# Score pass of a graph layer: squares and weighted one-hots moved between ScalarE and VectorE

## The reference, cut to what matters

```
proj_s = feature @ W_s.T;  proj_t = feature @ W_t.T
z = proj_s[src] + proj_t[dst];  z = where(z >= 0, z, 0.2 * z)
e = (z @ W_attn.T)[:, 0]
e_exp = exp(e - m[src]);  denom = segment_sum(e_exp, src)
...
def instance_norm(t):                 # t: keys or values, 64 channels per head
    mu = mean(t, -1);  var = mean((t - mu) ** 2, -1)
    return (t - mu) * rsqrt(var + EPS)
dots = einsum('bhnd,bhne->bhde', instance_norm(k), instance_norm(v))
```

## Time and profile before

| what | us |
|---|---|
| three runs, median | 2702.7 |
| lowest and highest | 2688.93 and 2711.46 |
| the profiled execution's own time | 2693.4 |
| its span, first to last instruction | 2691.6 |
| score pass in it, first gather at 168.0, last merge at about 1552 | 1384 |

### The profile page before, as it was taken

The page is one execution under the profiler, slowest core; times in us unless marked ns, Lnnn a source line. Parts: engine busy times, 40 slices in busy tenths (PEclk is TensorE's granted clock), DMA queues, the critical chain, the costliest instruction groups (busy, mean ns, idle before and its releaser), DMA issues. The chain is left out here.

```text
span 2691.6 us, 40213 instructions
## 1 busy us (share of the span) xinstructions
PE 2176.4 (81%) x10331; PEld 1518.2 (56%) x10331; DVE 1615.4 (60%) x6311; ACT 917.9 (34%) x3931; POOL 1289.2 (48%) x1316
## 2 busy tenths in 40 slices
PE   8966776777777677767777789999999959999998
PEld 5633444444444344434444478888788846666665
DVE  7834665655666565656656668777777843334443
ACT  6731333333333333333323324444334422221111
POOL 0035556555655555555555246566556622222222
PEclk9976778787878777877778789999989969999999
DMA  7855666666666666666666467666666741222220
GB/s 227 259 182 162 182 193 186 180 191 175 191 175 199 175 184 191 186 189 176 189 179 192 118 180 246 214 212 211 201 207 213 219 167 63 78 70 72 81 71 8
DMA packets 275757, 457.24 MB, mean 170 GB/s; under 512 B 58240, under 2 KB 199842, under 8 KB 275404
## 3 DMA queue, kind: packets, MB, share of 16 engines
q0 software_dynamic: 75920, 224.24, 29.3%
q1 hardware_dynamic: 199612, 230.49, 27.7%
HBM read 346.55 MB, written 113.74 MB: 171 GB/s over the span
## 5 line engine op out<-in xcount | busy, mean ns | idle before, releaser
L832 POOL DMA_INDIRECT pool_mem<-node_tab,edges x592 | 583.4, 985 | 592.0 <-issue 326.0
L963 PE MATMUL psum<-x_all 32*128 32x258 f32 x1568 | 266.7, 506 | 226.0 <-DVE x_all L1084 120.0
L1799 PE MATMUL psum<-x_all,pool_mem 128*128 128x256 f32 x1568 | 381.3, 397 | 21.4 <-DVE pool_mem L1999 13.1
L1608 POOL DMA_INDIRECT x_all<-node_tab,edges x294 | 295.1, 1004 | 165.0 <-issue 61.2
L1799 PEld LDWEIGHTS psum<-x_all,pool_mem 128*128 128x128 f32 x1568 | 307.2, 199 | 72.4 <-DVE pool_mem L1999 14.7
L872 ACT ACTIVATE x_all<-score_all,neg_max 128x8 f32<-128x8 f32 x98 | 29.7, 303 | 807.5 <-issue 419.1
L1098 DVE TENSOR_TENSOR pool_mem<-psum,pool_mem 128x258 f32<-128x258 f32 x296 | 114.9, 421 | 301.3 <-remote 165.3
L963 PEld LDWEIGHTS psum<-x_all 32*128 32x128 f32 x1568 | 115.8, 218 | 310.1 <-DVE x_all L1084 148.8
L1091 DVE SCALAR_TENSOR_TENSOR x_all<-psum,pool_mem 128x258 f32<-128x258 f32 x392 | 155.4, 422 | 177.3 <-remote 111.4
L996 PE MATMUL psum<-wkvT,x_all 128*128 128x512 f32 x392 | 233.7, 728 | 30.1 <-remote 13.0
L832 POOL DMA_INDIRECT x_all<-node_tab,edges x192 | 189.5, 987 | 141.7 <-DMA kept_rows<-x_all 81.3
(11 more groups left out here) (258 smaller groups left out, 3870.1 us busy)
## 6 DMA issues: line engine op xcount, KB each, us to landing
x_all<-kept_rows SPq DMA_DIRECT2D x98, 640.0 KB
kept_rows<-pool_mem SPq DMA_DIRECT2D x74, 640.0 KB
x_all<-in_L_ffn_w_dram SPq DMA_DIRECT2D x16, 1024.0 KB
kept_rows<-x_all SPq DMA_DIRECT2D x24, 640.0 KB
node_tab<-pool_mem SPq DMA_DIRECT2D x49, 258.0 KB, 3.1
x_all<-proj_t SPq DMA_DIRECT2D x392, 32.2 KB
pool_mem<-node_tab,edges POOLq DMA_INDIRECT x592
moe_in<-zeros SPq DMA_DIRECT2D x32, 258.0 KB, 4.2
```

What stands on the lines that cost most here:

```text
L832: g.indirect_dma_start(source_rows(r, u, ZW + D), None, node_tab, bass.IndirectOffsetOnAxis(ap=edges[:, 0, HALF * k + u:HALF * k + u + 1], ...
L963: mm = pe.matmul(psum[:, Z_BANK[q], 0:ZW], hot_T[h][rows_q, j * P:(j + 1) * P], t_win[rows_q, h, :], start=True, stop=(pair in BY_VECTOR), ...
L1608: g.indirect_dma_start(rows_g[k % R3][:, u - KEEP, 0:n], None, node_tab, bass.IndirectOffsetOnAxis(ap=edges[:, 0, HALF * k + u:HALF * k + ...
L1799: pe.matmul(psum[:, bank, 0:D], wide_picked[:, HALF * (k % 2) + u, :], row, start=((odd == 1 or m == 0) and n == 0), stop=(n == HALF - 1 a ...
```

## The change

Three edits, all in the score pass.

1. **Weighted one-hots.** ScalarE's 8 copies with a scale (L878) are gone. VectorE makes the same 128x512 tile by one multiplication of `hi_w` with the exp values broadcast over 64 columns (`values(k)`). It stands between `weigh_sum(k + 1, 5)` and `lo_hots(k, 1)`, so ahead of `hot(k + 2)`. Waits on `s_vexp` count one per half and not eight.
2. **Squares.** ScalarE squares a whole 128x512 bank by one instruction with no sum; 16 instructions with their 16 sums per tile become 2.
3. **Sums of squares.** VectorE sums them per head by `tensor_reduce`, 128x8 from 128x512 (`head_sums`), two per tile: the keys' one at the end of an odd half, behind `hot` and ahead of the next half's first `add_row`; the values' one in step 0 of `mix_norms`, followed by a wait for its own result.

```diff
@@ ScalarE, step(k)
-                        wait(act, s_vexp, HALF * (k - 1))
+                        wait(act, s_vexp, k - 1)
                         act.activation(expo_w[h], score_all[...], ACT.Exp, bias=...).then_inc(s_exp, 1)
                         act.activation(scale_w[h], ...).then_inc(s_ex2, 1)
-                        wait(act, s_hot, 3 * k + 2)
-                        wait(act, s_tab, k - 1)
-                        wait(act, s_exp, k + 1)
-                        for u in range(HALF):
-                            act.activation(vals[h][:, u, :], hi_w[h][:, u, :], ACT.Copy, scale=expo_w[h][:, u:u + 1]).then_inc(s_vexp, 1)
@@ ScalarE, square(i, j)
-                        for q in range(HEADS):
-                            act.activation(squares_w[:, j, q * DH:(q + 1) * DH], psum[:, 4 + j, q * DH:(q + 1) * DH], ACT.Square,
-                                           accum_out=head_sq[:, j, q:q + 1]).then_inc(s_sq, 1)
+                        act.activation(squares_w[:, j, :], psum[:, 4 + j, :], ACT.Square).then_inc(s_sq, 1)
@@ TensorE, tables(k)
-                        wait(pe, s_vexp, HALF * k + HALF)
+                        wait(pe, s_vexp, k + 1)
@@ VectorE
+                    def values(k):
+                        h = k % 2
+                        wait(v, s_hot, 3 * k + 2)
+                        wait(v, s_tab, k - 1)
+                        wait(v, s_exp, k + 1)
+                        v.tensor_tensor(vals[h], hi_w[h], expo_w[h].unsqueeze(2).to_broadcast([P, HALF, HIS]), ALU.mult).then_inc(s_vexp, 1)
+
+                    def head_sums(i, j):
+                        wait(v, s_sq, 2 * i + j + 1)
+                        wait(v, s_red, i)
+                        dve.done(v.tensor_reduce(head_sq[:, j, :], squares_w[:, j, :].rearrange("p (h d) -> p h d", d=DH), AX.X, ALU.add))
@@ VectorE, mix_norms(i, 0)
-                            wait(v, s_sq, 2 * HEADS * (i + 1))
+                            head_sums(i, 1)
+                            dve.wait()
                             v.tensor_scalar(head_var, head_sq, 1.0 / DH, LN_EPS, ALU.mult, ALU.add).then_inc(s_red, 1)
@@ VectorE, the loop over k
                         mix(k, 8, 9)
+                        values(k)
                         lo_hots(k, 1)
...
                         if k % 2 == 0:
                             mix_values(k // 2)
+                        elif k // 2 + 1 < PASSES:
+                            head_sums(k // 2 + 1, 0)
```

More of the change, by code:

```diff
@@ L1127, in hi_hots @@
                         hi = attr[:, 1, HALF * k:HALF * (k + 1)].unsqueeze(2).to_broadcast([P, HALF, HIS])
-                        wait(v, s_vexp, HALF * (k - 1))
+                        wait(v, s_vexp, k - 1)
                         v.tensor_tensor(hi_w[k % 2], hi, count[:, 0:HIS].unsqueeze(1).to_broadcast([P, HALF, HIS]), ALU.is_equal).then_inc(s_hot, 1)
+                    def values(k):
[8 more added lines that the diff above has]
+                        dve.done(v.tensor_reduce(head_sq[:, j, :], squares_w[:, j, :].rearrange("p (h d) -> p h d", d=DH), AX.X, ALU.add))
                     def merge(k):
@@ L1172, in _ @@
                     hot(1)
+                    head_sums(0, 0)
                     weigh_sum(0, 0)
```

## The result

The change took 2658.1 us (median of 4 runs, 2653.1 to 2666.1), against 2695.8 for the kernel before (4 runs, 2676.9 to 2711.5). The ratio is 0.985, with a 95% interval from 0.981 to 0.989: about 40 us less, where 43 more were forecast. The time lies outside the range that was given, on the other side.

The account below looks back on a forecast made before the run. The pass was taken as bound by TensorE and VectorE waiting for each other; 35 + 21 + 9 - 8 - 14 = +43 us gave a median of 2746 us, with 8 in 10 between 2680 and 2815.

Parts of the forecast that it names:

- I cost their removal at nothing: Removing ScalarE's 8 scaled copies, 2.02 us a half, gains 0 us, since they lie off the path.
- the pair of credits: Shorter squares cut VectorE's waits at L1141 (13 us, counted as 8) and TensorE's at L996 for x or keys (14 us).
- VectorE's terms: Added path time: `values` ahead of `hot` 35 us, the values' sum opening the even half 21, the keys' sum behind `hot` 9.
- The reading of the ring: In the score pass TensorE makes columns, VectorE weighs them and ends with `hot`, TensorE starts the next; this sets the pace.
- The prices: Time per new instruction: `values` 0.69 us, a reduction over 512 elements 0.69 us, a 128x512 square on ScalarE 0.63 us.
- The mark: Sign of the forecast: TensorE's `expand` waits for `hot` more often than 47 times or longer than 110 us.
- The other mark: Sign for ScalarE's queue as releaser: the remote waits of `add_row` shrink by far more than 50 us.
- the ScalarE case: Rival: `add_row`'s unknown-releaser waits hang on ScalarE's queue and shrink 1.08 us each, 54 us over the pass; 2650 us, chance 0.12.
- What lies behind the pass must not move: Sign: stages after the score pass keep their time, while the pass itself grows by about 43 us from 1384.
- No change: Rival: VectorE's 472 idle us of 1200 absorb its new work and credits cancel the rest; 2703 us, chance 0.26.
- The clock: Rival: longer pauses lower TensorE's granted clock in the pass from 0.77 to 0.73, 54 us on top; 2800 us, chance 0.10.
- The change doesn't do what it says: Rival: the edits don't take effect as described; only the price of a reduction over 8 groups could be off; no separate chance.

Follow-up runs that it names:

- light ScalarE: Kernel before without scaled copies (plain one-hots) and sums of squares, one square per bank, norm on a constant: ratio 0.975 (2681.1 us); on a 2280 us chip 1.001.
- heavy VectorE: Kernel before plus VectorE's new multiplication and reductions, results unused, ScalarE keeping all its work: ratio 1.003 (2746.6 us); on a 2280 us chip 1.013.

## Why the prediction was wrong

**The step that failed** is the first of the sum: "I cost their removal at nothing; what hides them is ScalarE's own idle time." Its twin is the pair of credits, which put 27 us on all that ScalarE's lighter work could bring. The light ScalarE measured 69 us on a 2700 us chip. And `values` with the scaled copies removed saved 32 us, although by the sum it should have cost 35. The sum was wrong at both ends: it counted 22 us for ScalarE's lighter work where 69 were measured, and 65 for VectorE's where the run below measured 8. That ScalarE stands idle for 394 + 294 us was true, and says nothing of when its next piece is ready; why it matters there is open (below).

**VectorE's terms** were 35 + 21 + 9 = 65 us. The new work alone measured 8 us (1 to 15) on a 2700 us chip. With a light ScalarE it may cost more: the ratio of the light ScalarE is 0.975 and that of the change 0.985, which would be 28 us, but these two come from different chips. The three terms were not measured apart on such a chip. All three take the share 58/98, the number of halves in which TensorE was seen to wait for `hot`; the run shows that a wait seen in a half does not mean that work ahead of it adds its full time.

**The reading of the ring** went further than its row. The 164 us of `add_row` are put down to "remote", not to TensorE; the waits that do name TensorE's columns (L973 and L963) are 82.6 us in 42 cases and 30.3 in 20. So the longest wait of the ring had no known releaser from the start.

**The prices** were right: 686 and 677 ns for 0.69, 586 ns for 0.63. VectorE's added work is 134 us, and 118 where the 0.08 us in which two instructions overlap counts once; the sum had 125. The cycle table of the Trainium skill (VectorE: DVE Perf Modes, errata section) gives 0.59; the trace doesn't agree, with 686. The same section says under the table that this row comes out too short, and its formula for an fp32 `tensor_tensor` gives 0.69 at 512 elements; with that the trace agrees.

**What was to show it.** TensorE's waits for `hot` grew as forecast, from 110 to 160 us, and the pass still got shorter. The mark came true and proves nothing: with the light ScalarE, where VectorE has no new work, TensorE waits for `hot` 141 us in 65 cases (300 to 1500 us, on another chip), nearly as in the change.

```profile
PE psum L955 <- DVE x_all L1075: 140.7, 65, 9.3
```

The other mark, the "remote" waits of `add_row`, fell from 164 to 81 us, and by the prediction's words "the ScalarE case holds". But the runs don't bear that mark out either. On one chip, from 300 to 1500 us, the light ScalarE (2681 us) and the heavy VectorE (2747 us) have these rows:

```profile
DVE pool_mem L1089 <- remote: 131.1, 39, 9.1
```

```profile
DVE pool_mem L1100 <- remote: 111.5, 28, 8.0
```

The faster kernel has the longer waits of this name. "What lies behind the pass must not move" failed too: from the last `merge` to the experts' first transposes the kernel before needs 2214.3 - 1552.2 = 662.1 us and the change 2187.4 - 1542.9 = 644.5. That stage's code is unchanged, and in the other profiles of 2700 us chips it takes from 664 to 677 us, whatever the pass ahead of it. So of the 27 us between the first two profiles only some 10 lie in the pass, and one pair of profiles can't place a gain of 1.5%.

**The rivals.** *No change* (0.26) is out on both kinds of chips, by the intervals. The busiest engine by matmul time is no guide here: TensorE has 88% of the span on a 2280 us chip, its list doesn't change, and the kernel got 1.4% slower. The Trainium skill (Perfetto Trace Analysis, Identifying the Most-Contended Engine) takes the engine with the highest occupancy, and for TensorE not the matmul time but, among others, its weight loads. In the pass of a 2280 us chip that names VectorE: 80%, against 75% for GpSimd and 52% for the weight loads. The trace doesn't agree: the engine that never waits there is GpSimd. *Faster through ScalarE's queue* (0.12, 2650 us) named the right engine, and a time 8 us from the one measured. Its mechanism isn't shown: it hung on the squares that stand ahead of the copy of x. The scaled copies aren't among them, and their removal saves as much. *The clock* is out: 0.77 before and after. *The change doesn't do what it says* is out by the instruction counts.

**On the 2280 us chips** a loss of about that size did come: 28 to 33 us more, where the sum said 43. That is luck and not the mechanism. The sum charged 65 us for work in a ring that GpSimd follows; here GpSimd follows nobody, and the loss is that its gathers take longer beside VectorE's new work. The credits are worth nothing for the same reason: L1141's waits for the squares are there too (14.5 us over the run), and taking them away brought nothing.

**What stays open.** Why ScalarE's instructions cost time on a 2700 us chip, though it idles. One place in the profile of the kernel before shows a wait that isn't for ScalarE's work itself, its timeline from 1122 us (start, us, what, idle before it):

```profile
1122.20 0.64 ACT L893 COPY x_all<-psum 128x512 f32<-128x512 f32 x1
1123.33 0.41 ACT L882 COPY x_all<-xn_all 128x256 f32<-128x256 f32 x1 [0.49 <-issue]
...
1127.69 2.90 PE L996 MATMUL psum<-wkvT,x_all 128*128 128x512 f32 x3 [5.40 <-remote]
...
1129.17 0.76 DVE L1098 TENSOR_TENSOR pool_mem<-psum,pool_mem 128x258 f32<-128x258 f32 x2 [8.71 <-remote]
```

The copy of x ends at 1123.74, and TensorE starts the matmul that needs it 3.9 us later; VectorE and TensorE stand meanwhile, with no releaser in the trace. The last section has what the trace shows of the queues.

## What to carry to other kernels

Idle time of an engine doesn't prove that its work is free: before costing a removal at nothing, look whether the waits have a releaser at all. If a large part of them is "issue" or "remote" (here 394 and 164 us of 1200), the profile doesn't explain the time, and both ends of the range must allow for that. Busy shares don't name the engine that sets the pace either: GpSimd is busy 75% of the pass on a 2280 us chip, less than TensorE and VectorE, and is the one that never waits. So go through the waits of every engine, and look for the one that has none. And a gain of 1 or 2% from work moved between two engines holds for the chip that it was measured on: repeat both kernels on a second chip before keeping the change.

## What the runs showed of the hardware

The same kernel takes 2280 us on some chips and 2696 to 2756 on others, and each kind repeats within its set (2276.5 to 2285.8 in one, 2722.7 to 2751.5 in another). Nearly the whole difference lies in two stages. The pass ends at 1198 instead of 1552 us; the stage behind it takes 604 us instead of 662. The last stage does not differ. The experts' first transposes in the kernel before, on a 2700 and on a 2280 us chip:

```profile
L2596 PE MATMUL psum<-ident,pool_mem x128: 272/273/477, 2214.3 to 2626.5; 128*128 128x128 f32 x128
```

```profile
L2596 PE MATMUL psum<-ident,pool_mem x128: 272/273/477, 1802.5 to 2216.6; 128*128 128x128 f32 x128
```

From the first to the last of them it is 412.2 and 414.1 us. The pass is unrolled and joins five engines by semaphores; the experts' stage is a loop in which TensorE is busy 398 of 412 us. The durations of the engines' instructions in the pass are alike too: `L878` takes 334 ns on both, `L832` 985 and 981. GpSimd is busy with the gathers of the pass for 773 and 774 us. What differs is its waits: on the 2280 us chip none is over 0.32 us, on the 2700 us chip 113 are, up to 11.9 us, and beyond the 0.30 us of each they come to 330 us. That is the whole difference of the pass up to its last gather (1340 us from first to last start, and 1012). They are put down mostly to ring slots, whose rows are not yet stored (147 and 81 us) or not yet read by VectorE (100 and 28):

```profile
  DMA kept_rows<-pool_mem: 147.1, 42
  DVE pool_mem L1098: 100.1, 34
  DMA kept_rows<-x_all: 81.3, 20
  DVE x_all L1091: 27.8, 10
```

Why those who empty the slots are late on the one kind and never on the other is open. One thing that differs is the queues' own steps. SyncE's steps at L1334 and L1333 wait for nothing (shortest, median and longest ns), on a 2700 us chip:

```profile
L1334 SPq FUSED_REGOPS  x392: 2/42/1302, 169.1 to 1527.4; - x196
L1334 SPq MOVE x_all<-proj_t x392: 3/29/1398, 169.2 to 1527.5; - x196
L1333 SPq SEQ_ASSERT  x392: 2/18/709, 169.0 to 1527.3; - x196
```

and on a 2280 us chip:

```profile
L1334 SPq FUSED_REGOPS  x392: 42/42/48, 169.5 to 1171.5; - x196
L1334 SPq MOVE x_all<-proj_t x392: 29/29/43, 169.6 to 1171.6; - x196
L1333 SPq SEQ_ASSERT  x392: 18/18/18, 169.4 to 1171.4; - x196
```

The medians are the same, but a register step of 42 ns takes up to 1.3 us on the one kind, and never over 48 ns on the other. That fits waits without a releaser on every engine, and a kernel that gains when ScalarE has 1677 instead of 3931 instructions to take in. It is an argument and not shown: no run on a 2700 us chip changed the number of instructions and left their work alone.

On a 2280 us chip the clock is granted at 0.88 in the pass instead of 0.77, and GpSimd starts a gather each 1.25 us where nothing lengthens it. Two of them follow here:

```profile
712.47 0.95 POOL L832 DMA_INDIRECT pool_mem<-node_tab,edges  x1 [0.30 <-issue]
713.72 0.95 POOL L832 DMA_INDIRECT pool_mem<-node_tab,edges  x1 [0.30 <-issue]
```

Eight of them are 10.0 us of a half of 10.5 (1030 / 98). The rest is mostly the gathers over 1000 ns. On a 2700 us chip, at 14.1 us a half (1384 / 98), a longer gather can take the place of a wait, which fits that the same VectorE work costs 30 us on the one kind and 8 on the other; it was not tried apart.
